# Order of VectorE's work in a unit of a batch-axis softmax attention

## The reference

```
Q, K, V = xn @ W.T + b, split into 16 heads of 8
scores  = einsum('bqhd,bkhd->hbqk', Q, K)
attn    = softmax(scores, axis=1)        # over the 32 batches
heads   = einsum('hbqk,bkhd->bqhd', attn, V)
```

## Time and profile before

| what | value |
|---|---|
| time, median of 3 | 1938.74 us |
| profiled execution, its own time | 1949.29 us |
| its span, first to last instruction | 1947.5 us |
| mean granted TensorE clock | 0.876 |
| TensorE matmul busy | 1522.9 us (78%) |
| VectorE busy | 1370.7 us (70%) |
| GpSimd busy | 1053.3 us (54%) |
| ScalarE busy | 924.6 us (47%) |

### The profile page before, as it was taken

One profiled execution on the slowest core, in us unless ns is written; L12 is line 12 of the kernel. 1 busy time (PEld: TensorE's weight loads), 2 busy tenths in 40 slices (PEclk: granted clock), 3 DMA queues, 4 the chain that ended last, 5 costly groups with the idle time before them and its releaser, 6 DMA issues. The chain is left out here.

```text
span 1947.5 us, 46207 instructions
## 1 busy us (share of the span) xinstructions
PE 1522.9 (78%) x14800; PEld 1113.8 (57%) x14801; DVE 1370.7 (70%) x3007; ACT 924.6 (47%) x1453; POOL 1053.3 (54%) x682
## 2 busy tenths in 40 slices
PE   4555389989898989899936995988889809999960
PEld 3334255545554555455526995666666609999960
DVE  6888499989898989799944663776777753333336
ACT  2222088878787878688812442212212204444430
POOL 5555057767676767677772442354445554444430
PEclk8767599999999989899967997987888859999985
DMA  3332533334343444243035332122222112222238
GB/s 110 110 107 97 199 72 79 72 73 76 68 81 68 78 66 80 60 79 66 23 77 148 100 87 73 53 71 73 66 81 65 40 50 65 65 66 66 62 106 281
DMA packets 116361, 163.74 MB, mean 84 GB/s; under 512 B 21104, under 2 KB 81776, under 8 KB 111600
## 3 DMA queue, kind: packets, MB, share of 16 engines
q1 hardware_dynamic: 82464, 110.85, 24.3%
q0 software_dynamic: 13600, 28.45, 4.5%
q10 hardware_dynamic: 20144, 22.32, 3.3%
HBM read 99.52 MB, written 62.01 MB: 83 GB/s over the span
## 5 line engine op out<-in xcount | busy, mean ns | idle before, releaser
L919 POOL TENSOR_TENSOR V<-Ex,R 128x4096 f32<-128x4096 f32 x64 | 480.0, 7500 | 252.1 <-DVE R L820 252.0
L888 ACT ACTIVATE Ex<-pB 128x512 f32<-128x512 f32 x512 | 551.6, 1086 | 132.2 <-PE pB L722 127.0
L792 DVE TENSOR_REDUCE mg<-pA 128x128 f32<-128x1024 f32 x256 | 301.7, 1207 | 76.8 <-PE pA L705 75.4
L814 DVE TENSOR_REDUCE Z<-Ex 128x64 f32<-128x2048 f32 x128 | 290.8, 2274 | 5.7 <-ACT Ex L888 5.6
L732 PE MATMUL pO<-V,Vh 128*8 128x128 f32 x4096 | 210.1, 282 | 43.7 <-ACT Oev L879 29.7
L722 PEld LDWEIGHTS pB<-qk 72*128 72x128 bf16 x2048 | 161.1, 99 | 127.4 <-issue 9.5
L1070 POOL DMA_INDIRECT y_d<-x1yb,x1xb x136 | 130.6, 960 | 152.8 <-issue 83.1
L705 PE MATMUL pA<-qk 72*128 72x128 bf16 x2048 | 165.4, 226 | 51.5 <-DMA qk<-ks_d 21.6
L722 PE MATMUL pB<-qk 72*128 72x128 bf16 x2048 | 202.7, 222 | 0.0
L717 PE MATMUL pB<-mh,identb 128*128 128x512 bf16 x512 | 201.8, 394 | 0.9 <-ACT Ex L888 0.2
L717 PE MATMUL pB<-ml,identb 128*128 128x512 bf16 x512 | 198.0, 387 | 0.0
(11 more groups left out here) (227 smaller groups left out, 2678.6 us busy)
## 6 DMA issues: line engine op xcount, KB each, us to landing
qk<-qs_d SPq DMA_DIRECT2D x288, 64.0 KB
qk<-ks_d SPq DMA_DIRECT2D x288, 64.0 KB
x1xb<-xs_d SPq DMA_DIRECT2D x136, 64.5 KB
f_ye<-y_d SPq DMA_DIRECT2D x16, 512.0 KB, 5.8
qs_d<-parts ACTq DMA_DIRECT2D x16, 384.0 KB, 2.6
ks_d<-parts ACTq DMA_DIRECT2D x16, 384.0 KB, 3.2
x0xb<-xs_d SPq DMA_DIRECT2D x72, 64.5 KB
xn_d<-xn SPq DMA_DIRECT2D x16, 258.0 KB, 3.2
```

The costliest lines, as they stand in the source:

```text
L792: dve.tensor_reduce(mg[:, :, g], pA[:, g % 2, :, :].rearrange("p b q -> p q b"), AX.X, ALU.max).then_inc(b_red, 1)
L814: dve.tensor_reduce(Z[:, q], Ex[:, j, q, :], AX.X, ALU.add).then_inc(b_sum, 1)
L888: act.activation(Ex[:, j, :, BG * g:BG * (g + 1)].rearrange("p q b -> p b q"), pB[:, g % 2, :, :], ACT.Exp).then_inc(b_exp, 1)
L919: pool.tensor_tensor(En[:, j % 2, :, :].rearrange("p b q -> p q b"), Ex[:, j, :, :], R[:, j % 2, :].unsqueeze(2).broadcast_to([P, P, B]), ...
```

## The change

VectorE's order in the body of a unit was: maximum 0, first half sum, maxima 1, 2 and 3, unit maximum, second half sum, low part, reciprocal. It becomes: maximum 0, first half sum, maximum 1, second half sum, reciprocal, maxima 2 and 3, unit maximum, low part. No instruction is added or taken away, and no wait is edited.

```diff
                             half_sum(v, vj, 0)
                         if more:
                             group_max(u + 2, 1)
+                        if summed:
+                            half_sum(v, vj, 1)
+                            inverse(v, vj)
+                        if more:
                             group_max(u + 2, 2)
                             group_max(u + 2, 3)
                             unit_max(u + 2)
-                        if summed:
-                            half_sum(v, vj, 1)
-                        if more:
                             low_part(u + 2)
-                        if summed:
-                            inverse(v, vj)
```

## The result

The changed kernel takes 2024.62 us (median of four, 2023.39 to 2030.01) against 1940.31 us before: ratio 1.0416, 95% interval 1.0387 to 1.0445. That is +84 us where +26 was forecast. The sign was right, the size was off by a factor of three, and the range (to 1981) missed it. The chips used later differ in speed (the kernel before takes 1886 to 1947 us on them), so every experiment is told by its ratio to the kernel before on its own chip. The totals in the expectations of e1 to e7 and e5b are for the first chip.

The account below looks back on a forecast made before the run. VectorE and TensorE were taken to nearly tie, TensorE pacing the kernel before. Interval growth 26.5 us, plus 3.1 at unit 1, minus 3.5 at the end: +26.1 on 1938.7, giving 1964.8 us; range 1948 to 1981.

Parts of the forecast that it names:

- Two engines nearly tie: Attention stage: TensorE paces two units at 22.25 us, VectorE needs 21.52, leaving VectorE 0.37 us slack per unit.
- The round trip costs 1.40 us from unit maximum to low part: VectorE's low part, waiting for ScalarE's high part, starts 1.40 us after the unit maximum; VectorE's period becomes 11.64 us.
- a sign of being wrong: Low part idling behind ScalarE 1.1 us or more, or under 0.3, would refute the round trip; about 0.7 expected.
- the 26 intervals without evacuation: Unstalled high-part intervals without evacuation: 3 grow by 0.88 us each, 23 by 0.99, to 11.64; 25.4 us.
- Each interval with evacuation becomes 11.64 us: The 28 high-part intervals with a product copy-out grow from 11.60 to 11.64 us, +1.1 us in all.
- sign of being wrong in the tie: Intervals still alternating with and without evacuation would refute the tie; uniform reciprocals 11.6 us apart outside stalls were expected.
- The stalled intervals stay: Five intervals with a stall at the loop's branch, every eight units, keep their length: 0 us.
- Unit 1's high part comes 3.1 us later: Unit 1: second sum and reciprocal now precede its unit maximum, moving the high part from 257.35 to 260.41.
- 3.5 us gained at the end: Stage's end: the earlier reciprocal lets GpSimd's last multiplies start earlier, until the last reciprocal limits them; 3.5 us saved.
- The first (ScalarE busy): ScalarE still in an exponential when the unit maximum ends; 1.84 instead of 1.40 us, total 1988.6; chance 0.12.
- Not slower: TensorE stays the bound, all intervals stay and only the end's gain remains; total 1935.2; chance 0.06.
- the stalls shrank: Loop-branch stalls absorbed by TensorE's new idle time, saving an estimated 30 us, total 1935; chance 0.04.

Follow-up runs that it names:

- e1: Kernel before, with the low part directly behind the unit maximum and second half sum and reciprocal still late; ratio 1.0305.
- e7: Changed kernel, with the low part taken up behind the next unit's first group maximum and two buffers for the maxima; ratio 1.0150.
- e5b: Kernel before, with ScalarE copying the product out before its high part; ratio 0.9919.
- e2: Kernel before, with only reciprocal and low part exchanged, so the reciprocal directly follows the second half sum; ratio 1.0004.
- e5: Changed kernel, with ScalarE copying the product out before its high part instead of behind it; ratio 1.0122.
- e3: Kernel before, with ScalarE copying the product out twice, TensorE waiting for the second copy, and VectorE's order untouched; ratio 1.0533.
- e4: Changed kernel, with five dummy matmuls on TensorE ahead of its wait for the evacuation in every odd unit; ratio 1.0207.
- e6: Changed kernel, with TensorE doing a unit's second score group before its first product group; ratio 1.0134.

## Why the prediction was wrong

- *Two engines nearly tie; VectorE's slack is 0.37 us a unit.* Right. e2 put 0.13 us into it at no cost, and e1 and e5 show that 0.9 us does not fit.
- *The round trip costs 1.40 us from unit maximum to low part.* Right for intervals in which ScalarE is early: idle time 0.72 to 0.81 us, and 11.70 us a unit against the 11.64 worked out. Behind an interval lengthened by the clock it was 1.31 to 1.36 us, with ScalarE still in an exponential, past the 1.1 us that the prediction had named as a sign of being wrong. That hardly lengthened the next interval, which stayed at 11.70 to 11.88 where no stall was in it. Right in size too: +28.0 us for the 26 intervals without evacuation, forecast 25.4.
- *Each interval with evacuation becomes 11.64 us (+1.1 us in all).* This is the step that failed: +51.2 us. The intervals still alternate (11.70 and mostly 13.1 to 14.6), the prediction's own sign of being wrong in the tie. The failure has two halves. The prediction compared two deadlines, 11.60 and 11.64, and took the later. But ScalarE's copy stands behind its wait for the unit maximum, so the wait that the change creates (1.0 us) is added to the 1.0 us of the evacuation: 2.06 to 2.23 us. The sentence "A new idle of 1.0 us is no longer than the evacuation waits (longest 1.1)" compared two pieces of idleness that lie end to end. This half costs no time by itself: the interval at 425.06, with 2.06 us of waiting and the clock at 1.00, lasts 11.70 us. The second half does: the prediction treated idleness as time only. TensorE's clock fell behind 22 of the 23 long waits, and slow matmuls stretch an interval in which ScalarE and TensorE had 0.04 us to spare. e3 shows that such a wait does this alone; e4 and e6 that shortening it brings the intervals with evacuation back to 11.70 us, but for one and three of 28; e5 that taking it away leaves about the forecast.
- *The stalled intervals stay.* Nearly: 81.4 for 88.8 us. They vary between kernels, from 81.4 to 94.4 us in the traces here.
- *Unit 1's high part comes 3.1 us later.* It moved from 257.35 to 259.76, by 2.4 us.
- *3.5 us gained at the end.* Wrong. From the last high part to the start of the last multiply it took 991.17 - 951.01 = 40.2 us; now 1066.62 - 1025.29 = 41.3. The rows are GpSimd's last two multiplies (L918) and the last reciprocal:

```profile
1058.25 7.26 POOL L918 TENSOR_TENSOR V<-Ex,R 128x4096 f32<-128x4096 f32 x1 [1.27 <-PE pO L732]
...
1063.45 0.95 DVE L820 RECIPROCAL R<-Z 128x128 f32<-128x128 f32 x1
...
1066.62 7.16 POOL L918 TENSOR_TENSOR V<-Ex,R 128x4096 f32<-128x4096 f32 x1
```

The reciprocal is ready at 1064.40, but the last multiply comes directly behind the one before it and its scatter, and that one waited 1.27 us for a product group: the multiply of unit u writes a buffer that the product group of unit u-2 must have read. GpSimd's waits were put down to VectorE before (172.7 us) and are put down to TensorE now (252.0 us). An earlier reciprocal only changes what GpSimd waits for. I had left that wait (`b_pv`) out.
- *Rivals.* The first (ScalarE busy) is what e1 shows, with ScalarE the late engine. "Not slower" did not occur; the stalls shrank by 7.4 us, where that rival had 30. No rival held the clock, though the stalls in the trace of before had shown it: the first score group behind the stall at 606.96 took 1.03 us, where an undisturbed one takes 0.62.

Open: why the clock falls behind one wait and not behind an almost equal one, and why it then stays down once for a 13.1 us interval and once for a 16.1 us one. The runs show that the fall comes more often with a longer wait, not what decides a single one. What the pauses inside product groups are is open too. It is also not shown how much of e4's remaining 0.8% above e5 is the filler itself; in the profiled execution e4's intervals with evacuation, but for one, are as short as e5's, and the five stalled ones take 92.5 us, e5's 82.9.

## What to carry to other kernels

When an instruction on engine A starts to wait, list what is queued behind it on A and add that wait to the one that the third engine already has there; do not compare the two. If the third engine is TensorE, price the sum twice: as idle time, and as matmuls at the lower clock behind it. Putting an independent copy ahead of the wait, or a ready score group ahead of TensorE's, was a gain even in the kernel that had no such loss.

## What the runs showed of the hardware

- TensorE's clock fell behind waits shorter than the loop's stalls (2.9 to 5.9 us in the kernel before). Counting intervals with evacuation in which the mean granted clock was below 1: waits of about 1.0 us, none of 28 (the kernel before); 1.48 to 1.57 us, 3 of 23 (e6); 1.41 to 1.58 us, 8 of 23 (e7); 2.06 to 2.23 us, 22 of 23 (the changed kernel); 1.99 to 2.29 us, 23 of 28 (e3). A fall costs 0.5 to 4.5 us per interval here.
- Idle time of TensorE can be worth filling with useless work: 1.24 us of dummy matmuls in every second unit took the ratio from 1.0416 to 1.0207.
- A half sum whose follower waits for it takes 2.31 us from start to start (1031.68 to 1033.99 in the changed kernel) against 2.19 with a follower that does not wait. The follower that waits is a reciprocal in all of these rows. The Trainium skill, "VectorE: DVE Perf Modes", section "The DRAIN you can't avoid", says for a chain of copies that a semaphore after each costs nothing extra; this trace disagrees, by 0.12 us.
